# One decoder layer on one core: the cross mask as rows of the score products, self stacks in row halves, expert weights per tile

## The reference

```python
scores = jnp.einsum('bhqd,bhkd->bhqk', q, k) / np.sqrt(D_K)
scores = jnp.where(mask[:, None, :, :] == 0, jnp.float32(-1000000000.0), scores)
p_attn = jax.nn.softmax(scores, axis=-1)
```

## Time and profile before

| | |
|---|---|
| median of three runs | 1160.65 us |
| the profiled execution's own time | 1154.14 us |
| its span | 1152.4 us |
| mean granted PE clock | 0.953 of 2.4 GHz |
| busy PE / PEld | 992.5 / 760.0 us |
| busy DVE / ACT / POOL | 748.2 / 802.7 / 603.0 us |
| DMA | 144 MB, 125 GB/s over the span |

### The profile page before, as it was taken

How to read it: one execution, slowest core, us unless ns; L and a number is a source line. 1 busy time by engine, 2 the same in 40 slices (tenths; PEclk the granted TensorE clock), 3 DMA queues, 4 the chain that set the end, 5 groups by cost and what they waited for, 6 DMA issues and landing times.

```text
span 1152.4 us, 31418 instructions
## 1 busy us (share of the span) xinstructions
PE 992.5 (86%) x11621; PEld 760.0 (66%) x11621; DVE 748.2 (65%) x2099; ACT 802.7 (70%) x1652; POOL 603.0 (52%) x825
## 2 busy tenths in 40 slices
PE   2467889999999999999999999899889999999900
PEld 1255667777777777777777777576657678888800
DVE  2654655666676666666666667356648988888816
ACT  2144466777777777777777777667779899999900
POOL 4313332446555556546546554445557666666750
PEclk9966999999999999999999999999999999999955
DMA  3336674635644745565456343464112354332229
GB/s 89 80 88 146 159 165 92 164 97 145 176 108 119 181 116 130 136 146 147 115 145 163 105 122 103 104 192 111 53 43 69 92 172 126 120 100 76 66 69 371
DMA packets 109313, 144.06 MB, mean 125 GB/s; under 512 B 23117, under 2 KB 87456, under 8 KB 104360
## 3 DMA queue, kind: packets, MB, share of 16 engines
q1 hardware_dynamic: 97816, 120.25, 40.5%
q0 software_dynamic: 9168, 17.21, 4.8%
q10 hardware_dynamic: 2176, 4.59, 1.1%
HBM read 88.30 MB, written 55.36 MB: 125 GB/s over the span
## 4 chain that ended last, share of the span: by engine, by line
PE 68%; DVE 8%; DMA 6%; issue 5%; ACT 5%; SPq 4%; POOL 3%; DVEq 0%; POOLq 0%; ACTq 0%
PE pv L1610 10%; PE sc_a L1591 9%; PE sc_m L1575 8%; PE wb L1565 5%; PE wb L1559 5%; PE sc_a L1596 5%; PE wb L1554 4%; PE sc_m L1580 3%; PE pv L1838 2%; PE pv L1831 2%; PE pv L1832 2%; DMA big<-y_d 2%; DVE negm_m L1084 2%; PE wb L1776 2%; PE wb L1645 1%
## 5 line engine op out<-in xcount | busy, mean ns | idle before, releaser
L839 ACT ACTIVATE probs<-sc_a 77x512 f32<-77x512 f32 (+1 forms) x512 | 300.6, 592 | 139.5 <-PE sc_a L1596 86.2
L1084 DVE TENSOR_REDUCE negm_m<-sc_m 128x4 f32<-128x512 f32 x256 | 169.7, 683 | 76.8 <-PE sc_m L1575 76.1
L633 POOL DMA_INDIRECT y_d<-yo,row x156 | 165.8, 1063 | 90.3 <-issue 38.9
L1084 DVE TENSOR_REDUCE negm_cm<-sc_m 128x4 f32<-128x308 f32 x256 | 119.3, 472 | 132.4 <-PE sc_m L1580 132.1
L624 POOL DMA_INDIRECT xs_d<-xrow,slot_i x128 | 133.4, 1042 | 98.6 <-PE sc_a L1596 51.7
L1610 PE MATMUL pv<-probs,big 128*32 128x128 f32 x4096 | 165.5, 280 | 0.6
L1575 PE MATMUL sc_m<-kbig,qbig 96*128 96x128 bf16 x1024 | 104.2, 228 | 35.9 <-DMA kbig<-stk_k 14.0
L1610 PEld LDWEIGHTS pv<-probs,big 128*32 128x32 f32 x4096 | 96.1, 109 | 55.3 <-ACT probs L839 26.7
L1287 DVE TENSOR_TENSOR gl<-g,gh 128x512 fp32r<-128x512 f32 x156 | 107.1, 689 | 35.7 <-ACT g L987 35.4
L1575 PEld LDWEIGHTS sc_m<-kbig,qbig 96*128 96x128 bf16 x1024 | 70.8, 101 | 80.3 <-issue 53.0
L1591 PE MATMUL sc_a<-qbig,kbig 102*128 102x128 bf16 x1024 | 100.7, 222 | 1.2 <-ACT probs L839 1.2
(11 more groups left out here) (218 smaller groups left out, 2388.8 us busy)
## 6 DMA issues: line engine op xcount, KB each, us to landing
xg<-xs_d SPq DMA_DIRECT2D x39, 260.0 KB, 2.7
stk_q<-parts_q SPq DMA_DIRECT2D x16, 384.0 KB, 2.9
stk_k<-parts_k SPq DMA_DIRECT2D x16, 384.0 KB, 2.6
qbig<-stk_q SPq DMA_DIRECT2D x16, 384.0 KB
kbig<-stk_k SPq DMA_DIRECT2D x32, 192.0 KB
stk_cq<-parts_cq SPq DMA_DIRECT2D x16, 384.0 KB, 2.9
cbig<-stk_cq SPq DMA_DIRECT2D x16, 384.0 KB
xin<-x_dram SPq DMA_DIRECT2D x16, 256.0 KB
```

Of the source, the lines that this page charges most:

```text
L633: nc.gpsimd.indirect_dma_start(out=y12_d, in_=yo[i % NY][:, c, :], in_offset=None, bounds_check=2 * B * S - 1, oob_is_err=False, out_offse ...
L839: nc.scalar.activation(probs[e % 4][0:rows], sc_a[e % 2][0:rows], ACT.Exp, scale=scale)\
L1084: nc.vector.tensor_reduce(out=negm[n][:, s, HG * g + 4 * half:HG * g + 4 * half + 4], in_=sc_m[u % 2][:, 0:4 * cols].rearrange("p (j k) -> ...
```

## The change

**Cross scores.** The cross stacks get 125 rows (CS = 77 + 48), 128 with the maxima (CR). Rows 0 to 76 of K hold a 77 x 77 identity for each head and sequence, written once by POOL (`places`); rows 0 to 76 of Q hold the transposed mask bias `mbT` (77 x 512), which SP copies from SBUF to SBUF for each of 16 heads and each block, 77 x 16 pieces of 1 KB. The two mask matmuls of a unit go. Q and K both hold 16 heads, with no zeros between: three transfers each, of 24, 16 and 8 rows, twice as long as before. The mask comes transposed from the host; POOL's mask operation works on 77 partitions x 512 instead of 128 x 308 and stands ahead of `third("cq")`; it waits for the stack of the block before.

**Self scores.** Group 0 lies in rows 0 to 50, group 1 in rows 64 to 114; a matmul uses 48 or 51 rows of one half. K holds 8 slots like Q; no zeros, no presets. Q is stacked by six transfers (24, 16, 8 rows for each group) instead of three, K by six as before.

**Experts.** W1, W2 and the biases of an expert lie in one row block on the host (1032 floats per partition, 528 KB). `weights` goes; `load(i)` first brings tile i's weights into one of three places, when tile i-3's splits are done. ACT and DVE no longer read the table.

```diff
+GP = 64
+KM = GP + KS + 3
+CS = SC + KS
+CR = CS + 3
+WROW = FC * D + F + 8
+NW = 3
...
                 def stack(n, b, dst):
                     sp.wait_ge(dumped[n].sem, dumped[n].val(b))
-                    for place, skip in RUNS:
-                        left = 3 - skip
-                        if n in ("q", "cq"):
-                            row, view = H * place, stk[n][0:left].rearrange("c (i g j) t -> (c i g) j t", i=DH, g=NG)
-                            sp.dma_start(dst[row:row + H * left, :, :], view).then_inc(stacked[n].sem, 16)
-                        else:
-                            row, view = H * place, stk[n][skip:3].rearrange("c (i g j) t -> g (c i) j t", i=DH, g=NG)
-                            for g in range(NG):
-                                sp.dma_start(dst[row + g:row + H * left:NG, g * HG:(g + 1) * HG, :], view[g])\
-                                    .then_inc(stacked[n].sem, 16)
+                    for g in range(NG):
+                        if n == "k" and b < 2:
+                            sp.wait_ge(ident_ok.sem, 7)
+                            ones_under(n, dst, GP * g + KS, slice(0, HG))
+                        for place, skip in RUNS:
+                            left = 3 - skip
+                            some = slice(0, left) if n == "q" else slice(skip, 3)
+                            row, view = GP * g + DH * place, stk[n][some].rearrange("c (i g j) t -> g (c i) j t", i=DH, g=NG)
+                            sp.dma_start(dst[row:row + DH * left, :, :], view[g]).then_inc(stacked[n].sem, 16)
+                def stack_cross(n, b, dst):
+                    sp.wait_ge(dumped[n].sem, dumped[n].val(b))
...
+                    for place, skip in RUNS:
+                        left = 3 - skip
+                        some = slice(0, left) if n == "cq" else slice(skip, 3)
+                        row, view = SC + DH * place, stk[n][some].rearrange("c (i h) t -> (c i) h t", i=DH)
+                        sp.dma_start(dst[row:row + DH * left, :, :], view).then_inc(stacked[n].sem, 16)
+                    if n == "cq":
+                        sp.wait_ge(mb_ok.sem, mb_ok.val(b))
+                        sp.dma_start(dst[0:SC, :, :], mbT[:].unsqueeze(1).broadcast_to([SC, H, T])).then_inc(stacked[n].sem, 16)
...
                     if t == NB - 1:
-                        weights()
                         load(0)
                         load(1)
...
                 def load(i):
...
+                    if i >= NW:
+                        sp.wait_ge(bias_ok.sem, bias_ok.val(i - NW))
+                        sp.wait_ge(wl_ok.sem, wl_ok.val(i - NW))
+                        sp.wait_ge(vl_ok.sem, vl_ok.val(i - NW))
+                    e = sp.value_load(tab[0:1, 0, bass.ds(i, 1)], min_val=0, max_val=E - 1)
+                    sp.dma_start(wraw[i % NW], W12[bass.ds(e, 1)].rearrange("e p w -> p (e w)")).then_inc(w_in[i % NW].sem, 16)
...
                     if on_(t):
-                        third("cq", t)
-                        wait_block(pool, st_f["c"], t - 2)
+                        wait_block(pool, stacked["cq"], t - 1)
                         pool.wait_ge(mk_in.sem, mk_in.val(t))
...
-                        nc.gpsimd.tensor_scalar(out=mbias[par][:], in0=mk[:], scalar1=0.0, scalar2=MASKED,
-                                                op0=ALU.is_equal, op1=ALU.mult).then_inc(mb_ok.sem, 1)
+                        nc.gpsimd.tensor_scalar(out=mbT[:].rearrange("k (s p) -> k s p", s=NS), in0=mk[:], scalar1=0.0,
+                                                scalar2=MASKED, op0=ALU.is_equal, op1=ALU.mult).then_inc(mb_ok.sem, 1)
+                        third("cq", t)
-                def zeros(stacks, n):
...
+                def places():
+                    for tile in cks:
+                        nc.gpsimd.tensor_copy(tile[0:SC].rearrange("p h (s k) -> p (h s) k", k=SC),
+                                              identb[0:SC, 0:SC].unsqueeze(1).broadcast_to([SC, H * NS, SC]))\
+                            .then_inc(preset["ck"].sem, 1)
...
+                def operands(n, half, g, shift):
+                    if n in ("m", "s"):
+                        return slice(GP * g, GP * g + KS + 3 * shift), 4 * half
+                    return slice(0, CR if shift else CS), HG * g + 4 * half
...
-                    if bias:
-                        i = nc.tensor.matmul(sc_m[u % 2][:, 0:4 * cols], identb[:],
-                                             bias[:, s, :].unsqueeze(1).broadcast_to([128, 4, cols]),
-                                             start=False, stop=True, skip_group_check=True)
...
-                    if bias:
-                        i = nc.tensor.matmul(sc_a[u % 2][0:cols, :], bias[:, s, :],
-                                             identb[:].unsqueeze(1).broadcast_to([128, 4, S]),
-                                             start=False, stop=True, skip_group_check=True)
```

More of the change, by code:

```diff
@@ L179, in program, with stacks @@
         rest["ck"] = sa("rest_ck", [128, TC])
-        def stacks(tile, at, heads):
-            n = (H if heads == H else HG)
-            cols = {H: TC, HG: T}[heads]
-            return [tile[0:KM, at + i * n * cols:at + (i + 1) * n * cols].rearrange("p (h t) -> p h t", h=n) for i in range(2)]
-        ks = [kbig[0:KM, i * H * T:(i + 1) * H * T].rearrange("p (h t) -> p h t", h=H) for i in range(2)]
-        qs = stacks(qbig, 0, HG)
-        cks, cqs = stacks(cbig, 0, H), stacks(cbig, 2 * H * TC, HG)
+        def stacks(tile, at, rows, heads, cols):
+            return [tile[0:rows, at + i * heads * cols:at + (i + 1) * heads * cols].rearrange("p (h t) -> p h t", h=heads)
+                    for i in range(2)]
+        qs, ks = stacks(qkbig, 0, KM, HG, T), stacks(qkbig, 2 * HG * T, KM, HG, T)
+        cks, cqs = stacks(cbig, 0, CR, H, TC), stacks(cbig, 2 * H * TC, CR, H, T)
         negm = {n: sa(f"negm_{n}", [128, NS, H]) for n in ("m", "cm")}
@@ L224, in over @@
             return nc.alloc_sbuf_tensor_at(name, list(shape), dt, offset=place_of[old] + k * TS * 4)[:]
-        wf = kbig[:].bitcast(F32).rearrange("p (e j f) -> p e j f", e=E, j=2)
-        wh, wl, vh, vl = ([over(f"{n}{i}", "qbig", 2 * k + i) for i in range(2)] for k, n in enumerate(("wh", "wl", "vh", "vl")))
+        raw = over("wraw", "qkbig", 8, F32, (128, NW * WROW))
+        wraw = [raw[:, i * WROW:(i + 1) * WROW] for i in range(NW)]
+        wh, wl, vh, vl = ([over(f"{n}{i}", "qkbig", 2 * k + i) for i in range(2)] for k, n in enumerate(("wh", "wl", "vh", "vl")))
         g, gh = ([over(f"{n}{c}", "big", FC * k + c, dt) for c in range(FC)] for k, (n, dt) in enumerate((("g", F32), ("gh", F32R))))
@@ L293, in program @@
         tab_ok, table_step, iotas, base_seen = sem("tab_ok"), sem("table_step"), sem("iotas"), sem("base_seen")
-        w_in, fill_st = sem("w_in", 16), sem("fill_st", 16)
+        w_in, fill_st = [sem(f"w_in{i}", 16) for i in range(NW)], sem("fill_st", 16)
         def follow(old, per):
@@ L464, in body @@
                             load(i)
-                def weights():
-                    sp.wait_ge(st_f["s"].sem, st_f["s"].val(NB - 1))
-                    for half in range(2):
-                        some = range(half * (E // 2), (half + 1) * (E // 2))
-                        sp.dma_start(wf[:, some[0]:some[-1] + 1, 0, :], W1[some[0]:some[-1] + 1].rearrange("e d f -> d e f"))\
-                            .then_inc(w_in.sem, 16)
-                        for e in some:
-                            sp.dma_start(wf[:, e, 1, :].rearrange("p (c d) -> p c d", c=FC),
-                                         W2[e].rearrange("(c f) d -> f c d", f=128)).then_inc(w_in.sem, 16)
                 def load(i):
@@ L765, in empty_tile @@
                         .then_inc(fill_ok.sem, 1)
-                steps(pool, body, {-3: lambda: zeros(ks, "k"), -2: numbers, -1: first_spare})
+                steps(pool, body, {-2: numbers, -1: first_spare})
                 def odds(b):
@@ L932, in squares @@
                         s, a = 2 * half + k, (D + E) * k
-                        i = nc.scalar.activation(sq_junk[:, s, :], wb[half][:, a:a + D], ACT.Square,
+                        i = nc.scalar.activation(on["c"][:, s].rearrange("p h i -> p (h i)"), wb[half][:, a:a + D], ACT.Square,
                                                  accum_out=ss[:, s:s + 1])
```

118 lines of the change are left out of this document (50 added, 68 removed).

## The result

The changed kernel took 1278.35 us (median of 4 runs, 1271.20 to 1282.08) against 1161.72 us for the kernel before beside it: 1.0995 times as long, 95% interval 1.0937 to 1.1053. The forecast was 1175 us with a range up to 1214. The sign was right; the size, +117 us instead of +14, was not.

What follows compares the result with a forecast made beforehand. PE was taken to bound both phases, with SP's transfer chain next. Twelve steady steps +6, start +13.6 and end -5.7 us made +13.9, so 1160.65 + 14 = 1175 us; range over the cases 1117 to 1214.

Steps and rivals of the forecast that it cites:

- rival (b): Clearly slower, chance 0.22: copy and halves delay the cm fold 9 us, clock falls in every Y phase, 1206 us.
- Cross stacks: the same bytes in half the rows ... I take 1.0: X phase, SP's queue: cross stacks in half the rows land 1.0 us later, bounds 0 and 2 us.
- less 0.7 for fewer issues: X phase, SP's queue: three transfers of K fewer to issue save 0.7 us, at most 1.9.
- The mask copy: X phase, SP's queue: copying 1.26 MB ahead of cross K's stack delays the cm fold 6.7 us, range 4.9 to 8.2.
- my bounds of 3.0 to 10.2: X phase: bounds in us on the cm fold's total delay, taken as 7.0 us.
- Mask products out, 5.8 us less 1.2 for ACT: Y phase: removing mask products saves PE 5.8 us, less 1.2 us waiting for ACT's exponentials; 19.1 us left.
- The clock, "in some steps it will come and in some not, 1.3 us": Y phase: slowed clock after PE's wait for the cm fold costs 1.3 us, range 0 to 3.1.
- Self stacks, "covered, just": Y phase: the m fold lands 18.3 to 20.8 us in, just covered by a phase of 20.4 us.
- POOL: Mask operation grows from 1.27 to about 2.1 us, moving into POOL's 2.81 us wait for ACT; nothing lost.
- Experts, "0 us": Expert tiles: loading weights per tile costs 0 us, each transfer being issued two tiles ahead.
- Start, +13.6: Start of the kernel: later folds and four early self stacks or folds, less Y-phase savings, add 13.6 us.
- End, -5.7: Steps 15 to 17: a fold 7.0 us later against Y-phase savings of 4.6, 4.6 and 3.5, -5.7 us.

Runs made afterwards that it cites:

- experiment 1: Changed kernel, but from block 2 on the mask copy moves one row instead of 77: 1196.55 us, 1.0299 times the kernel before.
- experiment 7: Kernel before, cross Q in six half-row transfers: 1168.80 us; changed kernel, cross rows in both partition halves: 1241.91 us, with a one-row mask copy 1161.47 us.
- experiment 3: Changed kernel with mask products again and 48 zero rows added, so cross products have 96 and 99 rows: 1263.94 us, 1.0884 times the kernel before.
- experiment 5: Changed kernel with only POOL's order changed, third("cq") back in front of the mask operation: 1280.84 us, 1.1018 times the kernel before.
- experiment 2: Changed kernel with the mask as products again, no mask copy, cross stacks of 48 and 51 rows: 1506.38 us, 1.2857 times the kernel before.

## Why the prediction was wrong

**The mechanism was the forecast's, the size was not even rival (b)'s.** The cm fold became late, PE idled in front of its first cross product, and the clock fell behind it. In the step shown: X phase 28.8 us against 25.1 forecast, Y phase 21.7 against 20.4. Rival (b) had named a clock fall in every Y phase and the partitions' place, with steps of 47.5 to 48.2; they are 51.1. Between forecast and the two profiled executions lie 114 us: 63 in the steady steps (69 for 6), 24 in the start (37.5 for 13.6) and 27 in the end (21 for -5.7).

**The step that failed: "Cross stacks: the same bytes in half the rows ... I take 1.0", less 0.7 for fewer issues.** That net +0.3 us (bounds -1.9 to +2.0) measures 3.8 (experiment 1), of which 2.8 are the place of the rows (experiment 7). I had priced the number of rows in a transfer, which costs 0.8 us for cross Q. Only (b) spoke of the place, and it named the self groups and the mask rows, not the cross stacks at 77 to 124 where it cost this. The saving of three issues did not come: the three of K took 6.65 us to issue, against 4.05 for six before. With the copy of one row in front of them they took 1.2 to 1.8 (experiment 1), so it is the copy that held them.

**The mask copy** was right: 5.6 us for 6.7 taken, within 4.9 to 8.2. Together 9.4 us instead of 7.0, inside my bounds of 3.0 to 10.2, so the bounds of the delay held and those of the time did not. In the step shown the rest of the X phase's +3.7 is 0.6 us by which I had set the chain's start too low and 0.7 in the fold's landing (3.2 us instead of 2.5). Past the cover every microsecond of delay is one of every step; my worst case had steps 3.2 us longer, measured are 6.3.

**Mask products out, 5.8 us less 1.2 for ACT:** near the 4.6 forecast. PE's work in a Y phase at full clock falls from 23.70 to 19.09 us, 4.6 (experiment 1), and experiment 3 against experiment 1 gives 4.2 a block. It was worth nothing net, since the copy that buys it costs 5.6 us of a chain with 3.2 to spare by the forecast, and 2.6 by the correction just named.

**The clock, "in some steps it will come and in some not, 1.3 us":** PE waited for the fold 13 times, 113.0 us in all; in the step shown 4.0 us at 0.50 and 4.0 at 0.96 lose 2.2 us, 0.9 above the term.

**Self stacks, "covered, just":** not quite. The m dump lands 7.9 us after its issue instead of 4.7, +3.2, where 1.9 for issues and up to 2.5 were allowed; alone it costs 0.6%. In the changed kernel it hardly gated, since the Y phase began so late (PE waited for the m fold twice in the whole run, 17.1 us). What I had not seen is a gain: PE's X work fell from 20.14 to 18.65 us.

**POOL:** right. The order is worth nothing (experiment 5), though the operation took 1.95 us (2.1 forecast) and its cover shrank from 2.81 us to 0.46.

**Experts, "0 us":** wrong by 9 us. The tiles as such kept PE busy; one tile near the fills did not, since its rows stood behind weights in the queue (4.5 us, and 0.8 with the rows first), and the last cm fold was already 4 us late, which I put down to the first loads. I had read one stretch of six tiles for 39.

**Start, +13.6:** measured 37.5 us to block 3. The first cm fold goes out at 164 us before, 170 with the self halves alone, 185 and 182 with the new stacks but mask products (experiments 2 and 3), 191 after. So 18 to 21 of these 27 us are stacks, not the mask; I had taken 1.9 us for each early self stack or fold and nothing for the cross stacks' place. The identity copies were not free either: see the last section. **End, -5.7:** +21, of which the weights are some 9. I can't divide the rest: the part behind the dump of block 15 alone takes 375.8 us in the kernel before and 386.8 with the self halves, whose tiles are the same.

## What to carry to other kernels

Before trading engine work for a copy, find the transfer chain's spare time in that phase: here some 3 us stood against 9.4 us of new transfers, and all of the excess was paid in every step, with a clock loss on top. Price a new layout of the destination by where its partitions lie, not by bytes and rows alone, and spread the rows of a transfer burst over both halves: that won 2.8 us for the cross stacks, though taking turns won the self stacks only 0.9. A late small transfer behind a large one, where the phase must wait for both, was cured here by fewer bytes, not by the copy's order or another queue. Where the large one is not due yet, order did help: the m dump ahead of K's stack ended the waits for the m fold. And a transfer put first moves the wait to the one behind it, as the rows ahead of the weights did.

## What the hardware showed

**Clock and rows of a product.** Cross products of 48 and 51 rows left the granted clock at 0.50 for 48 us of busy PE, and at means of 0.50 to 0.58 in five of eleven Y phases, 0.77 to 0.82 in the others. With zeros to make them 96 and 99 it was 0.89 to 0.93 in all eleven, in the one shown it rose within 8 us, and the kernel was 242 us shorter for the same results (1506.38 and 1263.94 us). Self products of 48 rows in the X phase did run at 1.00 when they alternated between rows 0 to 47 and 64 to 111.

**Two row halves at once.** Starts of products on the two halves stand 0.01 to 0.02 us apart, while each lasts 0.22 to 0.23 us. Eight of them take 0.34 us, from 586.71 to the next operation at 587.05; in the kernel before the same eight, which share rows, take 0.45 (507.13 to 507.58). In the X phase of the changed kernel, maxima products of one group beside shifted ones of the other:

```profile
586.71 0.23 PE L1580 MATMUL sc_m<-qkbig 48*128 48x128 bf16 x1
586.72 0.23 PE L1591 MATMUL sc_a<-qkbig 51*128 51x128 bf16 x1
586.77 0.22 PE L1580 MATMUL sc_m<-qkbig 48*128 48x128 bf16 x1
586.79 0.22 PE L1591 MATMUL sc_a<-qkbig 51*128 51x128 bf16 x1
```

**DVE beside a long POOL copy.** At the start, the two identity copies on POOL and a product of 8 x 128 values on DVE:

```profile
32.55 8.86 DVE L1460 TENSOR_SCALAR sim_u<-sim_n,sim_rn 8x128 f32<-8x128 f32 x1 [2.15 <-POOL sim_rn L754]
...
32.80 8.52 POOL L746 COPY cbig<-identb 77x4928 bf16<-77x4928 bf16 x2
...
41.46 2.06 DVE L1089 TENSOR_REDUCE negm_m<-sc_m 128x4 f32<-128x512 f32 x3
```

DVE's small operation ended just when POOL's copies did, and the first maxima began at 41.46 us; in the kernel before the same operation took 4.56 us and the maxima began at 38.55. POOL wrote zeros beside it there, 4.23 us from 33.34, and the DVE operation ended with them too. In experiment 2 POOL writes nothing at this place, and the operation takes 0.27 us:

```profile
32.69 0.27 DVE L1455 TENSOR_SCALAR sim_u<-sim_n,sim_rn 8x128 f32<-8x128 f32 x1 [2.15 <-POOL sim_rn L751]
```

So its length follows what POOL writes beside it, in three kernels. "POOL idles there" was true and not enough.
